# One sine product, scores ahead of values, and the softmax reciprocal spread by TensorE inside the output bank

## The chip, the cores and the metric

One Trainium2 chip, one of its cores. Five engines run their own instruction streams and meet at semaphores: TensorE (PE in the profile, its weight loads PEld), VectorE (DVE), ScalarE (ACT), GpSimd (POOL) and SyncE (SP), which issues DMAs here. The metric is the device time of the program in microseconds; lower is better.

## The reference, cut to what matters

The program is a stack of stages over 16 sequences of 256 tokens and 128 channels. The change touches the second stage, a transformer of six layers with local attention (16 heads of 64, window 32). The feed-forward half of a layer is left out here:

```python
qkv = shift_tokens(x) @ Wqkv            # x: (16, 256, 128), Wqkv: (128, 3 * 1024)
q = l2norm(q) * qs;  k = l2norm(k) * ksc
q = q * cos * scale + rotate_half(q) * sin * scale
k = k * cos * inv + rotate_half(k) * sin * inv
# windows of 32 queries see their own and the one before
sim = einsum('bhwie,bhwje->bhwij', bq, bk2) * 8
attn = softmax(where(mask, -max, sim))
out = einsum('bhwij,bhwje->bhwie', attn, bv2)
x = out @ Wo + x
x = ffn(shift_tokens(x)) + x
```

## The kernel before

Each stage (`phase_a`: first attention, `phase_b`: the six-layer transformer, `phase_c`: the state-space stage) is a software pipeline. In `phase_b` an item is one sequence in one layer, 6 x 16 = 96 items. A step of the pipeline works on four of them at once: the projection (front) of item n+1, the local attention of item n, output projection and layer norm (tail) of item n-1, the feed-forward of item n-2. A step has 16 slots, and every engine walks through them in the same order; what an engine does in a slot is written out by hand, and an engine waits only where a semaphore says so. An instruction that waits holds back all that is behind it on its engine.

Attention goes by pairs of heads, p = 0 to 7, one in each even slot. For pair p:

- slot 2p: PE `scores(p)`: the mask is put into the two score banks by a bf16 product (L799), then q times k for both heads (L803, L806). DVE takes the row maximum (L1093); ACT takes four exponentials with row sums into `ssum` (L955, L957). `scores(p)` waits for the exponentials of p-1.
- slot 2p+2: PE transposes the probabilities into `T_BANK` (L828, L829), ACT copies them to `PT` (L979); DVE turns the small block of the window before (L1089).
- slot 2p+4: PE `values(p)`: values times `PT` (L789, L793) into half of `O_BANK`; two pairs, a group, fill the bank.

The softmax denominators go by groups i of two pairs (GROUPS = 4): slot 4i+4, DVE, reciprocal of `ssum` (L1098) and its spreading to 64 columns a head, `rrep` (L1103, 128x512); slot 4i+5, PE, four transposes of `rrep` into `T_BANK` (L903); slot 4i+6, ACT, copy to `rb` (L975); slot 4i+7, DVE, `O_BANK` times `rb` into `oT` (L1084). Slots above 15 fall into the next step. So the first `values` of a group waits for the L1084 of the group before, and the probability transposes of that slot wait for the L975 that empties `T_BANK`.

In an even slot PE does, in this order, `values(p-2)`, `scores(p)`, the transposes of p-1, and then a piece of the projection of the next item (L845 to L847, 512 columns) and spare-bank work. ACT does the `rb` copy, the `PT` copy, the exponentials, and then the square of the projection piece into `sq` (L991) or its copy to `V`. DVE does L1084 (odd slots), L1089, L1093, the reciprocal work, and in the slot behind a q or k piece `rotate`: the cosine product (L1057), two half-wide sine products (L1060), the sum of squares (L1063). Pieces of q and k are in slots 1, 2, 4, 6, 8, 10, 12 and 13.

PE's other work: `WO_SLOT` 4 and 5, output projection, half in each (L859); first feed-forward product in slots 6, 8, 9 (L885), the second in slot 15 (L893); transposes of q and k in slots 10 to 13 and 0 to 3 (L776). ACT loads another function table for the GELU of slot 11 (L998) and loads the exponential's again in slot 12. DVE normalises in slots 15 and 1 (L1070).

Of the kernel before, what the change touches and what calls it, by code (L numbers as in the profile page):

```python
# [22 lines left out]
ALU = mybir.AluOpType  # L23
# [554 lines left out]
WO_SLOT = (4, 5)  # L578
# [4 lines left out]
PAIR_T, PAIR_PV = 2, 4  # L583
SPREAD_LAG, TURN_LAG, KEEP_LAG, SCALE_LAG = 4, 5, 6, 7
# [84 lines left out]
def phase_b(nc, g, d, ps):  # L669
    with ExitStack() as stack:  # L670
# [15 lines left out]
        s.rrep = s.sb("rrep", [P, TT, 4, DB]); s.rb = s.sb("rb", [P, 2, NT]); s.oT = s.sb("oT", [P, HPAIRS, NT])  # L686
# [9 lines left out]
        s.pv_done, s.rinv_ready, s.rrep_ready, s.rb_full, s.rb_ready, s.onorm = s.sems("pv_done rinv_ready rrep_ready rb_full rb_ready onorm")  # L696
# [56 lines left out]
        def _(pe):  # L753
            def body(step):
# [24 lines left out]
                def values(item, p, own):  # L779

                    pe.wait_ge(s.pt_ready, HPAIRS * item + p + 1)
                    pe.wait_ge(s.before_ready, HPAIRS * item + p + 1)
                    if p % 2 == 0:
                        wait(pe, s.onorm, GROUPS * item + p // 2)
                    pt, v = s.PT[:, p % 2], s.V[:, own]
                    at = p % 2 * NT
                    for j in range(2):
                        side, head = slice(j * DB, (j + 1) * DB), slice((2 * p + j) * DB, (2 * p + j + 1) * DB)
                        nc.tensor.matmul(ps[side, O_BANK, at:at + KEYS], v[:, 0, head], pt[:, j, 0:KEYS], start=True, stop=False,  # L789
                                         skip_group_check=True)  # L790
                    for j in range(2):
                        side, head = slice(j * DB, (j + 1) * DB), slice((2 * p + j) * DB, (2 * p + j + 1) * DB)
                        last = nc.tensor.matmul(ps[side, O_BANK, at + P:at + NT], v[:, 1, head], pt[:, j, KEYS:KEYS + P], start=False, stop=True,  # L793
                                                skip_group_check=True)
                    last.then_inc(s.pv_done, 1)
# [14 lines left out]
                for slot in range(SLOTS):  # L810
                    item, p = pair_at(step, slot, PAIR_PV)
                    if p is not None:
                        values(item, p, pa if slot >= PAIR_PV else 1 - pa)
                    elif step.attn and slot == 0:
                        for use in TRANSPOSE_SLOT.values():
                            bank, uses = step.spare_of_before(("tr", use))
                            pe.wait_ge(s.spare_free[bank], uses + 1)
                    if step.attn and slot % 2 == 0:
                        wait(pe, s.exp_done, HPAIRS * n + slot // 2)
                        scores(slot // 2)  # L820
                    item, p = pair_at(step, slot, PAIR_T)
                    if p is not None:
                        if not step.attn:
                            pe.wait_ge(s.exp_done, HPAIRS * item + p + 1)
                        if p % 2 == 0:
                            wait(pe, s.rb_ready, GROUPS * item + p // 2)
                        for j in range(2):
                            nc.tensor.transpose(ps[:, T_BANK, j * NT:j * NT + P], s.Pr[:, p % 2, j, 0:P], g.ident[:])  # L828
                            last = nc.tensor.transpose(ps[:, T_BANK, j * NT + P:(j + 1) * NT], s.Pr[:, p % 2, j, OWN], g.ident[:])  # L829
                        last.then_inc(s.t_done, 1)  # L830
# [79 lines left out]
        def _(act):  # L910
            act.wait_ge(s.zeroed, 1)

            def body(step):
# [47 lines left out]
                for slot in range(SLOTS):  # L961
# [8 lines left out]
                    item, i = group_at(step, slot, KEEP_LAG)  # L970
                    if i is not None:
                        act.wait_ge(s.rb_full, GROUPS * item + i + 1)
                        if not step.attn:
                            wait(act, s.onorm, GROUPS * item + i)
                        nc.scalar.activation(s.rb[:], ps[:, T_BANK].rearrange("p (a t) -> p a t", a=2), ACT.Copy).then_inc(s.rb_ready, 1)  # L975
# [27 lines left out]
        def _(dve):  # L1003
# [20 lines left out]
            def body(step):  # L1024
# [20 lines left out]
                def rotate(at):  # L1045
# [27 lines left out]
                for slot in range(SLOTS):  # L1073
# [5 lines left out]
                    item, i = group_at(step, slot, SCALE_LAG)  # L1079
                    if i is not None:  # L1080
                        dve.wait_ge(s.rb_ready, GROUPS * item + i + 1)
                        if not step.attn:
                            dve.wait_ge(s.pv_done, HPAIRS * item + 2 * i + 2)
# [11 lines left out]
                    item, i = group_at(step, slot, SPREAD_LAG)  # L1095
                    if i is not None:
                        heads = slice(4 * i, 4 * i + 4)
                        nc.vector.reciprocal(s.rinv[:, heads], s.ssum[:, heads]).then_inc(s.rinv_ready, 1)  # L1098
                        if not step.attn:
                            dve.wait_ge(s.rb_full, GROUPS * item + i)  # L1100
                        dve.wait_ge(s.rinv_ready, GROUPS * item + i + 1)
                        wide = s.rinv[:, heads].rearrange("p h (t o) -> p t h o", o=1).broadcast_to((P, TT, 4, DB))
                        nc.vector.tensor_tensor(s.rrep[:], wide, wide, ALU.max).then_inc(s.rrep_ready, 1)  # L1103
# [547 lines left out]
```

## Time and profile before

| | |
|---|---|
| median of 3 runs | 6295.01 us (6290.99 to 6296.99) |
| the profiled execution | 6296.2 us; its span from the first to the last instruction 6294.4 us |
| PE busy | 5301.7 us (84% of the span) |
| DVE, ACT, POOL busy | 4720.1 us (75%), 4122.9 us (66%), 3575.6 us (57%) |
| granted TensorE clock, mean | 0.941 of full speed |

Busy times are the union of an engine's instructions. Idle time of an engine counts only if what follows it on the chain that ends last came later by it. A timeline row gives the start in us from the span's start, the duration in us, engine, line and operation, what it writes and reads, and in brackets the engine's idle time ahead of it and what ended that. A matmul of f32 data is recorded as two instructions, a transpose as one; instructions of one line that follow each other are merged into one row (x4). The end of a matmul is modelled, so distances are taken from start to start.

### The profile page before, as it was taken

The numbers are of one execution on the slowest core, as the hardware profiler recorded it, in microseconds if no ns is written. First come the engines' busy times: TensorE is split into PE (matmuls) and PEld (weight loads), VectorE is DVE, ScalarE is ACT, GpSimd is POOL, SyncE is SP. The second block draws the span as 40 slices with busy tenths as digits, with TensorE's granted clock in tenths as the row PEclk, the third lists the DMA queues.
The fourth block names the chain that finished last, engine by engine and source line by source line (L and its number), as shares of the span: only waits on it lengthen the run. The fifth ranks groups of instructions, "written<-read, shape, count | busy, mean of one in ns | idle before, by whom it ended". The sixth has DMA issues, their size and how long they took to land. (4 is left out here: it accounts for less than half of the span.)

```text
span 6294.4 us, 111018 instructions
## 1 busy us (share of the span) xinstructions
PE 5301.7 (84%) x34984; PEld 3935.5 (63%) x34984; DVE 4720.1 (75%) x9586; ACT 4122.9 (66%) x12293; POOL 3575.6 (57%) x2277
## 2 busy tenths in 40 slices
PE   7999788888888888888888888888888888566666
PEld 6999666666666666666666666666666666333333
DVE  4666677777777787777777777777777776577777
ACT  3555467777777777777777777777777776454543
POOL 1222466666666666666666666666666664344444
PEclk9999899999999999999999999999999999688887
DMA  0000000000000000000000000000000000000000
GB/s 20 4 3 2 23 1 0 0 0 10 10 0 0 0 18 1 0 0 4 14 1 0 0 5 13 1 0 0 5 8 1 0 0 0 4 3 3 3 3 4
DMA packets 35417, 25.50 MB, mean 4 GB/s; under 512 B 11315, under 2 KB 29302, under 8 KB 35190
## 3 DMA queue, kind: packets, MB, share of 16 engines
q1 hardware_dynamic: 26302, 22.22, 1.2%
q8 instruction: 118, 1.93, 0.1%
q10 hardware_dynamic: 8888, 0.45, 0.1%
q14 instruction: 109, 0.89, 0.1%
HBM read 20.57 MB, written 2.10 MB: 4 GB/s over the span
## 5 line engine op out<-in xcount | busy, mean ns | idle before, releaser
L1155 POOL TENSOR_TENSOR b_w<-b_w,b_vt 128x512 f32<-128x512 f32 x768 | 986.7, 1285 | 1547.3 <-DVE b_ss L1063 1020.2
L1159 POOL TENSOR_TENSOR b_rn<-b_ssm,all_neg_half 128x16 f32<-128x16 f32 x384 | 1127.3, 2936 | 32.0
L979 ACT ACTIVATE b_PT<-ps 128x512 f32<-128x512 f32 x768 | 459.5, 598 | 978.4 <-PE ps L829 978.4
L1057 DVE TENSOR_TENSOR b_w<-ps,until_b_rotab 128x512 f32<-128x512 f32 x768 | 527.8, 687 | 648.3 <-ACT b_sq L991 643.7
L1093 DVE TENSOR_REDUCE b_nm<-ps 128x4 f32<-128x640 f32 x768 | 633.1, 824 | 235.1 <-PE ps L806 209.0
L955 ACT ACTIVATE b_Pr<-ps,b_nm 128x128 f32<-128x128 f32 x1536 | 564.4, 367 | 111.6 <-DVE b_nm L1093 109.8
L957 ACT ACTIVATE b_Pr<-ps,b_nm 128x160 f32<-128x160 f32 x1536 | 609.7, 397 | 0.0
L845 PE MATMUL ps<-b_Whi,b_xlo 128*128 128x512 f32 x1152 | 590.5, 513 | 19.0 <-DVE b_Wlo L1078 11.4
L789 PE MATMUL ps<-b_PT,b_V 128*64 128x160 f32 x3072 | 385.3, 328 | 244.9 <-DVE b_oT L1084 237.7
L1060 DVE TENSOR_TENSOR b_vt<-ps,until_b_rotab 128x256 f32<-128x256 f32 x1536 | 571.6, 413 | 0.0
L828 PE MATMUL ps<-all_ident,b_Pr 128*128 128x128 f32 x1536 | 439.1, 311 | 153.7 <-ACT b_rb L975 147.2
L1063 DVE TENSOR_REDUCE b_ss<-b_sq 128x8 f32<-128x512 f32 x768 | 517.9, 674 | 0.0
L991 ACT ACTIVATE b_sq<-ps 128x512 f32<-128x512 f32 x768 | 472.9, 616 | 12.1 <-PE ps L847 12.0
L799 PE MATMUL ps<-until_b_mask_bf,until_b_ident_bf 128*128 128x320 bf16 x1536 | 346.3, 308 | 143.9 <-ACT b_Pr L957 143.0
L776 PE MATMUL ps<-all_ident,b_w 128*128 128x128 f32 x3072 | 463.7, 280 | 3.0 <-DVE b_w L1070 3.0
L925 ACT ACTIVATE b_qkT<-ps 128x512 f32<-128x512 f32 x768 | 463.1, 621 | 0.6 <-PE ps L776 0.5
L847 PE MATMUL ps<-b_Whi,b_xhi 128*128 128x512 f32 x1152 | 460.2, 400 | 0.0
L846 PE MATMUL ps<-b_Wlo,b_xhi 128*128 128x512 f32 x1152 | 458.7, 398 | 0.0
L776 PEld LDWEIGHTS ps<-all_ident,b_w 128*128 128x128 f32 x3072 | 381.0, 145 | 96.2 <-ACT b_qkT L925 23.8
L828 PEld LDWEIGHTS ps<-all_ident,b_Pr 128*128 128x128 f32 x1536 | 222.1, 145 | 309.0 <-ACT b_rb L975 219.8
L789 PEld LDWEIGHTS ps<-b_PT,b_V 128*64 128x64 f32 x3072 | 158.7, 137 | 407.7 <-issue 348.9
L829 PE MATMUL ps<-all_ident,b_Pr 128*128 128x128 f32 x1536 | 397.0, 284 | 0.0
(256 smaller groups left out, 14155.0 us busy)
## 6 DMA issues: line engine op xcount, KB each, us to landing
b_Wraw<-in_L_ffn_Wqkv SPq DMA_DIRECT2D x36, 256.0 KB, 2.8
b_Wo<-in_L_ffn_Wo SPq DMA_DIRECT2D x6, 512.0 KB, 4.0
a_xtok<-in_L_attn_hidden_states SPq DMA_DIRECT2D x16, 128.0 KB, 2.1
out<-c_xout SPq DMA_DIRECT2D x16, 128.0 KB, 1.8
b_W<-in_L_ffn_W SPq DMA_DIRECT2D x6, 341.0 KB, 2.9
setup_wmod<-in_L_wmod SPq DMA_DIRECT2D x2, 384.0 KB
b_W<-in_L_ffn_W SPq DMA_DIRECT2D x6, 128.0 KB
setup_rot<-in_rot SPq DMA_DIRECT2D x1, 256.0 KB
```

Of the source, the lines that this page charges most:

```text
L776: last = nc.tensor.transpose(bank[:, i * P:(i + 1) * P], s.w[:, tt, c % 2, c // 2, i * P:(i + 1) * P], g.ident[:])
L789: nc.tensor.matmul(ps[side, O_BANK, at:at + KEYS], v[:, 0, head], pt[:, j, 0:KEYS], start=True, stop=False, skip_group_check=True)
L828: nc.tensor.transpose(ps[:, T_BANK, j * NT:j * NT + P], s.Pr[:, p % 2, j, 0:P], g.ident[:])
L845: nc.tensor.matmul(ps[:, F_BANK[k % 2]], s.xlo[:, pf, rows], s.Whi[:, cols], start=True, stop=False)
L955: nc.scalar.activation(s.Pr[:, p % 2, j, 0:P], ps[:, S_BANK[j], WIN:KEYS], ACT.Exp, bias=s.nm[:, h, 0:1], accum_out=s.ssum[:, h, 0:1])
L957: last = nc.scalar.activation(s.Pr[:, p % 2, j, P:], ps[:, S_BANK[j], KEYS:2 * KEYS], ACT.Exp, bias=s.nm[:, h, 1:2], accum_out=s.ssum[:, h ...
L1057: nc.vector.tensor_tensor(s.w[:, tt, c % 2, which].rearrange("p (h e) -> p h e", e=DB), rotated, g.rotab[:, bass.ds(lf, 1), 2 * which, tt] ...
L1060: last = nc.vector.tensor_tensor(turned[:, :, z], raw[:, :, 1 - z], sin[:, :, z * (DB // 2):(z + 1) * (DB // 2)].broadcast_to((P, 8, DB // ...
L1063: nc.vector.tensor_reduce(s.ss[:, j, which * 8:(which + 1) * 8], s.sq[:, i % 2].rearrange("p (h e) -> p h e", e=DB), AX.X, ALU.add).then_i ...
L1093: nc.vector.tensor_reduce(s.nm[:, 2 * p:2 * p + 2], ps[:, S_BANK[0]:S_BANK[1] + 1, 0:TT * KEYS].rearrange("p j (t k) -> p j t k", t=TT), A ...
L1155: nc.gpsimd.tensor_tensor(rows, rows, s.vt[:, i % 4], ALU.add).then_inc(s.pool_add, 1)
L1159: nc.gpsimd.tensor_tensor(s.rn[:, j], s.ssm[:, j], g.neg_half[:, 0:HB], ALU.pow).then_inc(s.pool_r, 1)
```

## The change

`scores(p)` is issued ahead of `values(p-2)` in an even slot. `O_BANK` now belongs to one pair: the values go to its columns 0 to 255, and behind them four more matmuls, two token halves by two heads, have the reciprocal's column, repeated 64 times by a step of 0, as stationary operand and the identity as moving one; they put the spread reciprocal into columns 256 to 511. For an even p they wait for the reciprocal (`rinv_ready`), which DVE makes in the same slot, now ahead of the row maximum. L1103, the L903 transposes, `rrep` and the waits on `T_BANK` for `rb` go. ACT copies `rb` for each pair (256 columns) in the slot of its values, ahead of the `PT` copy; DVE scales each pair (256 columns) in the odd slot behind. `values(p)` waits for the scaling of pair p-1. The two sine products become one of 512 columns whose PSUM operand is read with the half index reversed (a negative step). `WO_SLOT` goes from (4, 5) to (3, 4).

```diff
-WO_SLOT = (4, 5)
+WO_SLOT = (3, 4)
-PAIR_T, PAIR_PV = 2, 4
-SPREAD_LAG, TURN_LAG, KEEP_LAG, SCALE_LAG = 4, 5, 6, 7
+PAIR_T, PAIR_PV, PAIR_SCALE = 2, 4, 5
+RINV_LAG = 4
@@ PE, values(item, p, own)
-                    if p % 2 == 0:
-                        wait(pe, s.onorm, GROUPS * item + p // 2)
+                    wait(pe, s.onorm, HPAIRS * item + p)
...
+                    if p % 2 == 0:
+                        pe.wait_ge(s.rinv_ready, GROUPS * item + p // 2 + 1)
+                    for tt in range(TT):
+                        for j in range(2):
+                            side, at = slice(j * DB, (j + 1) * DB), NT + tt * P
+                            last = nc.tensor.matmul(ps[side, O_BANK, at:at + P], s.rinv[:, 2 * p + j, tt:tt + 1].broadcast_to((P, DB)), g.ident[:],
+                                                    start=True, stop=True, skip_group_check=True)
@@ PE, order in a slot
+                    if step.attn and slot % 2 == 0:
...
+                        wait(pe, s.exp_done, HPAIRS * n + slot // 2)
+                        scores(slot // 2)
                     item, p = pair_at(step, slot, PAIR_PV)
                     if p is not None:
                         values(item, p, pa if slot >= PAIR_PV else 1 - pa)
...
-                        if p % 2 == 0:
-                            wait(pe, s.rb_ready, GROUPS * item + p // 2)
...
-                            pe.wait_ge(s.onorm, GROUPS * t + 2 * half + 2)
+                            pe.wait_ge(s.onorm, HPAIRS * t + 4 * half + 4)
...
-                    item, i = group_at(step, slot, TURN_LAG)
-                    if i is not None:
-                        pe.wait_ge(s.pt_ready, HPAIRS * item + 2 * i + 2)
-                        pe.wait_ge(s.rrep_ready, GROUPS * item + i + 1)
-                        for p in range(2):
-                            for tt in range(TT):
-                                last = nc.tensor.transpose(ps[:, T_BANK, p * NT + tt * P:p * NT + (tt + 1) * P],
-                                                           s.rrep[:, tt, 2 * p:2 * p + 2].rearrange("p j e -> p (j e)"), g.ident[:])
-                        last.then_inc(s.rb_full, 1)
@@ ACT
-                        nc.scalar.activation(s.rb[:], ps[:, T_BANK].rearrange("p (a t) -> p a t", a=2), ACT.Copy).then_inc(s.rb_ready, 1)
+                    item, p = pair_at(step, slot, PAIR_PV)
+                    if p is not None:
+                        act.wait_ge(s.pv_done, HPAIRS * item + p + 1)
+                        nc.scalar.activation(s.rb[:, p % 2], ps[:, O_BANK, NT:2 * NT], ACT.Copy).then_inc(s.rb_ready, 1)
@@ DVE
-                    for z in range(2):
-                        last = nc.vector.tensor_tensor(turned[:, :, z], raw[:, :, 1 - z],
-                                                       sin[:, :, z * (DB // 2):(z + 1) * (DB // 2)].broadcast_to((P, 8, DB // 2)), ALU.mult)
-                    last.then_inc(s.dve_uv, 1)
+                    nc.vector.tensor_tensor(turned, raw[:, :, ::-1], sin.rearrange("p a (z e) -> p a z e", z=2).broadcast_to((P, 8, 2, DB // 2)),
+                                            ALU.mult).then_inc(s.dve_uv, 1)
...
-                        nc.vector.tensor_tensor(s.oT[:, 2 * i:2 * i + 2], ps[:, O_BANK].rearrange("p (a t) -> p a t", a=2), s.rb[:],
-                                                ALU.mult).then_inc(s.onorm, 1)
+                    item, p = pair_at(step, slot, PAIR_SCALE)
+                    if p is not None:
+                        dve.wait_ge(s.rb_ready, HPAIRS * item + p + 1)
+                        nc.vector.tensor_tensor(s.oT[:, p], ps[:, O_BANK, 0:NT], s.rb[:, p % 2], ALU.mult).then_inc(s.onorm, 1)
...
+                    item, i = group_at(step, slot, RINV_LAG)
+                    if i is not None:
+                        heads = slice(4 * i, 4 * i + 4)
+                        nc.vector.reciprocal(s.rinv[:, heads], s.ssum[:, heads]).then_inc(s.rinv_ready, 1)
...
-                        wide = s.rinv[:, heads].rearrange("p h (t o) -> p t h o", o=1).broadcast_to((P, TT, 4, DB))
-                        nc.vector.tensor_tensor(s.rrep[:], wide, wide, ALU.max).then_inc(s.rrep_ready, 1)
```

## Rows read from the trace of the kernel before

**Rows 1.** Busy time in the transformer stage: stretch, its length, busy us of each engine.

```profile
740.00:5356.00 4616.00, 4014.97 (x28483) 2986.45 (x28482) 3576.55 (x7751) 3320.66 (x10164) 2989.14 (x1901) 0.97 0.01 3
```

**Rows 2.** Waits of PE in the whole run: us in total, times, longest.

```profile
PE ps L789 <- DVE b_oT L1084: 237.7, 164, 3.0
...
PE ps L828 <- ACT b_rb L975: 147.2, 167, 1.3
PE ps L799 <- ACT b_Pr L957: 143.0, 98, 1.6
...
PE ps L903 <- DVE b_rrep L1103: 46.7, 59, 1.6
```

**Rows 3.** Timeline of PE, slots 10 and 12 of one step.

```profile
3061.14 0.27 PE L829 MATMUL ps<-all_ident,b_Pr 128*128 128x128 f32 x1
...
3063.61 0.49 PE L789 MATMUL ps<-b_PT,b_V 128*64 128x160 f32 x4
3063.94 0.39 PE L793 MATMUL ps<-b_PT,b_V 128*64 128x128 f32 x4
3064.26 0.44 PE L799 MATMUL ps<-until_b_mask_bf,until_b_ident_bf 128*128 128x320 bf16 x2
...
3065.33 0.33 PE L828 MATMUL ps<-all_ident,b_Pr 128*128 128x128 f32 x1
...
3065.71 0.27 PE L829 MATMUL ps<-all_ident,b_Pr 128*128 128x128 f32 x1
```

**Rows 4.** Timeline of ACT, slot 10: last of the exponentials.

```profile
3063.28 0.22 ACT L957 ACTIVATION_READ_ACCUMULATOR b_Pr<-ps,b_nm 128x1 f32 x1
```

**Rows 5.** Timeline of DVE, slots 11 and 12.

```profile
3064.11 0.69 DVE L1057 TENSOR_TENSOR b_w<-ps,until_b_rotab 128x512 f32<-128x512 f32 x1 [1.95 <-ACT b_sq L991]
3064.72 0.74 DVE L1060 TENSOR_TENSOR b_vt<-ps,until_b_rotab 128x256 f32<-128x256 f32 x2
3065.38 0.67 DVE L1063 TENSOR_REDUCE b_ss<-b_sq 128x8 f32<-128x512 f32 x1
3066.08 0.24 DVE L1089 STREAM_TRANSPOSE b_PT<-b_Pr 32x64 f32<-32x64 f32 x1
```

**Rows 6.** Timeline of PE, slots 0, 4, 6, 8 and 9.

```profile
3029.42 0.49 PE L789 MATMUL ps<-b_PT,b_V 128*64 128x160 f32 x4 [1.61 <-DVE b_oT L1084]
...
3032.09 0.42 PE L829 MATMUL ps<-all_ident,b_Pr 128*128 128x128 f32 x1
...
3040.60 0.49 PE L789 MATMUL ps<-b_PT,b_V 128*64 128x160 f32 x4 [1.34 <-DVE b_oT L1084]
...
3042.69 0.27 PE L829 MATMUL ps<-all_ident,b_Pr 128*128 128x128 f32 x1
...
3045.92 1.89 PE L859 MATMUL ps<-b_oT,b_Wo 128*128 128x256 f32 x8
...
3055.05 0.27 PE L829 MATMUL ps<-all_ident,b_Pr 128*128 128x128 f32 x1
...
3058.38 0.60 PE L903 MATMUL ps<-all_ident,b_rrep 128*128 128x128 f32 x4
```

**Rows 7.** Timeline of PE, slot 0 of the next step.

```profile
3077.24 0.49 PE L789 MATMUL ps<-b_PT,b_V 128*64 128x160 f32 x4 [1.61 <-DVE b_oT L1084]
```

**Rows 8.** Timeline of ACT, slot 12.

```profile
3067.50 0.59 ACT L979 ACTIVATE b_PT<-ps 128x512 f32<-128x512 f32 x1
...
3070.75 0.21 ACT L957 ACTIVATION_READ_ACCUMULATOR b_Pr<-ps,b_nm 128x1 f32 x1
```

**Rows 9.** Timeline of DVE, slot 0 of the next step.

```profile
3079.66 0.24 DVE L1089 STREAM_TRANSPOSE b_PT<-b_Pr 32x64 f32<-32x64 f32 x1
...
3080.68 0.19 DVE L1098 RECIPROCAL b_rinv<-b_ssum 128x8 f32<-128x8 f32 x1
```

**Rows 10.** Groups of DVE by line: count, busy us, mean ns, idle before.

```profile
L1084 DVE TENSOR_TENSOR b_oT<-ps,b_rb 128x512 f32<-128x512 f32 x384 | 261.0, 680 | 1.5 <-PE ps L793 1.5
```

**Rows 11.** Groups of ACT by line, same stretch and columns.

```profile
L946 ACT ACTIVATE b_hgate<-ps,b_lp 128x256 f32<-128x256 f32 x192 | 96.0, 500 | 11.5 <-PE ps L885 11.5
```

More of the change, by code:

```diff
@@ L685, in phase_b @@
         s.PT = s.sb("PT", [P, 2, 2, 2 * KEYS])
-        s.rrep = s.sb("rrep", [P, TT, 4, DB]); s.rb = s.sb("rb", [P, 2, NT]); s.oT = s.sb("oT", [P, HPAIRS, NT])
+        s.rb = s.sb("rb", [P, 2, NT]); s.oT = s.sb("oT", [P, HPAIRS, NT])
         s.lp = s.sb("lp", [P, 7]); s.lnp = s.sb("lnp", [P, 2])
@@ L695, in phase_b @@
             "clamp_done pool_r s_done max_done exp_done t_done pt_ready before_ready")
-        s.pv_done, s.rinv_ready, s.rrep_ready, s.rb_full, s.rb_ready, s.onorm = s.sems("pv_done rinv_ready rrep_ready rb_full rb_ready onorm")
+        s.pv_done, s.rinv_ready, s.rb_ready, s.onorm = s.sems("pv_done rinv_ready rb_ready onorm")
         s.lp_ready, s.lnp_ready, s.shifted, s.gelu_done, s.hg_ready, s.x_ready = s.sems("lp_ready lnp_ready shifted gelu_done hg_ready x_ready")
@@ L782, in values @@
                     pe.wait_ge(s.before_ready, HPAIRS * item + p + 1)
-                    if p % 2 == 0:
-                        wait(pe, s.onorm, GROUPS * item + p // 2)
+                    wait(pe, s.onorm, HPAIRS * item + p)
                     pt, v = s.PT[:, p % 2], s.V[:, own]
-                    at = p % 2 * NT
                     for j in range(2):
                         side, head = slice(j * DB, (j + 1) * DB), slice((2 * p + j) * DB, (2 * p + j + 1) * DB)
-                        nc.tensor.matmul(ps[side, O_BANK, at:at + KEYS], v[:, 0, head], pt[:, j, 0:KEYS], start=True, stop=False,
+                        nc.tensor.matmul(ps[side, O_BANK, 0:KEYS], v[:, 0, head], pt[:, j, 0:KEYS], start=True, stop=False,
                                          skip_group_check=True)
@@ L792, in values @@
                         side, head = slice(j * DB, (j + 1) * DB), slice((2 * p + j) * DB, (2 * p + j + 1) * DB)
-                        last = nc.tensor.matmul(ps[side, O_BANK, at + P:at + NT], v[:, 1, head], pt[:, j, KEYS:KEYS + P], start=False, stop=True,
-                                                skip_group_check=True)
+                        nc.tensor.matmul(ps[side, O_BANK, P:NT], v[:, 1, head], pt[:, j, KEYS:KEYS + P], start=False, stop=True,
+                                         skip_group_check=True)
+                    if p % 2 == 0:
[5 more added lines that the diff above has]
+                                                    start=True, stop=True, skip_group_check=True)
                     last.then_inc(s.pv_done, 1)
@@ L810, in body @@
                 for slot in range(SLOTS):
+                    if step.attn and slot % 2 == 0:
+                        if slot == 0 and step.tail is None:
+                            for use in TRANSPOSE_SLOT.values():
+                                bank, uses = step.spare_of_before(("tr", use))
+                                pe.wait_ge(s.spare_free[bank], uses + 1)
+                        wait(pe, s.exp_done, HPAIRS * n + slot // 2)
+                        scores(slot // 2)
                     item, p = pair_at(step, slot, PAIR_PV)
@@ L813, in body @@
                         values(item, p, pa if slot >= PAIR_PV else 1 - pa)
[L814 to L820, printed above, removed]
                     item, p = pair_at(step, slot, PAIR_T)
@@ L969, in body @@
                     read_spare(slot - 1)
[L970 to L974, printed above, removed]
-                        nc.scalar.activation(s.rb[:], ps[:, T_BANK].rearrange("p (a t) -> p a t", a=2), ACT.Copy).then_inc(s.rb_ready, 1)
+                    item, p = pair_at(step, slot, PAIR_PV)
+                    if p is not None:
+                        act.wait_ge(s.pv_done, HPAIRS * item + p + 1)
+                        nc.scalar.activation(s.rb[:, p % 2], ps[:, O_BANK, NT:2 * NT], ACT.Copy).then_inc(s.rb_ready, 1)
                     item, p = pair_at(step, slot, PAIR_T)
@@ L1078, in body @@
                             nc.vector.tensor_tensor(s.Wlo[:, cols], s.Wraw[:, k % RAW], s.Whi[:, cols].bitcast(F32), ALU.subtract).then_inc(s.w_ready, 1)
[L1079 to L1083, printed above, removed]
-                        nc.vector.tensor_tensor(s.oT[:, 2 * i:2 * i + 2], ps[:, O_BANK].rearrange("p (a t) -> p a t", a=2), s.rb[:],
-                                                ALU.mult).then_inc(s.onorm, 1)
+                    item, p = pair_at(step, slot, PAIR_SCALE)
+                    if p is not None:
+                        dve.wait_ge(s.rb_ready, HPAIRS * item + p + 1)
+                        nc.vector.tensor_tensor(s.oT[:, p], ps[:, O_BANK, 0:NT], s.rb[:, p % 2], ALU.mult).then_inc(s.onorm, 1)
                     item, p = pair_at(step, slot, PAIR_T)
@@ L1094, in body @@
                                                 AX.X, ALU.max, negate=True).then_inc(s.max_done, 1)
[L1095 to L1101, printed above, removed]
-                        wide = s.rinv[:, heads].rearrange("p h (t o) -> p t h o", o=1).broadcast_to((P, TT, 4, DB))
-                        nc.vector.tensor_tensor(s.rrep[:], wide, wide, ALU.max).then_inc(s.rrep_ready, 1)
                     if step.tail is not None and slot == RES_SLOT:
```

## The prediction

> **What bounds the kernel now.** I read the page's slices first: the transformer stage runs evenly between some 0.74 and 5.36 ms, so what happens to one of its steps happens about 94 times (96 items, the pipeline full for 94). In that stage PE is busy for 4015 of 4616 us, DVE for 3577, ACT for 3321, POOL for 2989 [rows 1]. PE is near its limit, but it does wait, and the view of waits tells for whom: the values for the scaling of the group before, 237.7 us; the transposes of the probabilities for the `rb` copy that still uses their bank, 147.2; the scores for the exponentials, 143.0; the turning of `rrep` for DVE, 46.7 [rows 2]. Together that is 575 us, 6 us a step. So there is something to win, and PE still has to be fed.
>
> Then the timeline of one whole step. From one slot-0 `values` to the next it takes 3077.24 - 3029.42 = 47.82 us [rows 6, 7]. The reader is to see how far DVE is behind PE: PE begins slot 12 at 3063.61 [rows 3], DVE gets to its first instruction of that slot, L1089, at 3066.08 [rows 5], 2.47 us later, because it had to do the rotation of slot 11 first, and that waited 1.95 us for ACT's square, which stands behind the exponentials. The same lag is in slot 0: PE at 3077.24 [rows 7], DVE at 3079.66 [rows 9]. Before the change that lag is harmless: in slot 12 PE wants from DVE only what was made in slots before.
>
> **The change part by part: PE's work.** A transpose of 128 f32 columns takes 0.11 us of PE; so L903 costs 4 x 0.11 = 0.43 a group. L793, two f32 matmuls of 128 columns in four instructions, begins 0.32 ahead of the mask; the L789 before it, with 160 columns, takes 0.33 without a change of array shape behind it, so L793's own work is 0.33 x 128/160 = some 0.21 to 0.26 (I take 0.21, two transposes' time) and 0.11 is the gap at the change from 64 stationary columns to 128 [rows 3]. The new matmuls are four of L793's kind: 2 x 0.21 = 0.43 a pair. Bounds: 0.43 if both halves of the array work side by side as L793's seem to, 0.86 if a repeated column loses that.
>
> Here a rule speaks against the change. The Trainium skill, TensorE: Matmul & The Clock Gate, section Terms, says that the transpose mode is four times faster for FP32, and the new matmuls spread the column without it. By that rule one of them would cost 4 x 0.11 = 0.44 and four, in side-by-side pairs, 0.88; the rows of L793 show a factor of two, and the sum goes by them.
>
> Order: before, an even slot changes array shape four times (values 64 columns, mask 128, scores 64 rows, transposes 128), after it three times, since values follow the scores directly: a gap of 0.11 less. PE's work a step: 8 x (0.43 - 0.11) - 4 x 0.43 = +0.8 us.
>
> **DVE and ACT.** L1103 goes, 0.69 us four times, where DVE was not late for anybody. L1084 (0.68 [rows 10]) becomes two of 256 columns, nearest the half-wide sine products, 0.33 apart: the same in all, but only one of them, some 0.28 shorter, stands in front of what follows in its slot. The single sine product should run like the 512-wide cosine product, 3064.72 - 3064.11 = 0.61 from start to start, where the two took 3065.38 - 3064.72 = 0.66 [rows 5]: 0.05 saved. The negative step is in no row; the bounds are 0 and twice the time (+0.6). I take 0.61, since the two halves already read PSUM out of order. ACT copies 256 columns eight times instead of 512 four times; nearest is L946, 0.50 [rows 11]. It stands ahead of the `PT` copy, but the transposes take longer to arrive than it, so it costs something only where ACT is late itself, in slot 12.
>
> **Waits that go, and the one that comes.** The `rb` wait of the transposes and the `rrep` wait are gone, and the scaling is wanted 1.07 us later in its slot, behind the scores. In their place PE waits, in slots 0, 4, 8 and 12, in front of the new matmuls, for a reciprocal that DVE makes in the same slot behind L1089. PE would be there 1.07 (scores, 3064.26 to 3065.33) + 0.54 (values) = 1.61 us after the start of the slot [rows 3]; DVE, at its present lag, 2.47 + 0.24 (L1089) + 0.19 (L1098 [rows 9]) + 0.08 (two starts, estimate) = 2.98 [rows 3, 5]. Behind the waiting matmul on PE are the transposes of the probabilities, behind these the `PT` copy, the exponentials, the square, the rotation, the L1089 of the next even slot, and the projection. So from such a matmul to the next it is a chain, and I price it, R being the first new matmul:
>
> - R to the last transpose: 0.43 + 0.10 + 0.38 (3065.33 to 3065.71) = 0.91. Slot start to last transpose: 1.61 + 0.91 = 2.52 [rows 3].
> - Last transpose to exponentials done: 3061.14 to 3063.28 + 0.22 = 2.36 [rows 3, 4].
> - Last transpose of a slot to the reciprocal of the next even slot seen by PE: 3066.08 - 3061.14 = 4.94, - 0.05, + 0.51 = 5.40 [rows 3, 5].
>
> Slot 0 to 4: 0.91 + 2.36 + 0.05 (the scores' start) + 2.52 + 5.40 = 11.24. The output projection's half that moves to slot 3 fits under the 5.40. Slot 4 to 8: 0.91 + PE's work up to slot 6 + 2.52 + 5.40. That work is 3042.69 to 3045.92 = 3.23 [rows 6]: the second half of the output projection, which began there, is now earlier. 12.06. Slot 8 to 12: work up to slot 10 is 3055.05 to 3058.38 = 3.33 [rows 6], 12.16. Slot 12 to 0: R at 3061.14 + 5.40 = 3066.54; ACT, held up by the GELU and two table loads, gets to the `PT` copy at 3067.50, now 0.50 later for `rb`, so its exponentials end at 3070.96 + 0.50 = 3071.46 [rows 8]; from there to L1089 of slot 0 it was 3079.66 - 3070.96 = 8.70 of DVE work [rows 8, 9], less 0.28 and 2 x 0.05, plus 0.51: R at 3080.29, 13.75. The sum is 49.21 against 47.82, +1.39 us. The table loads stay as they are.
>
> One term more: in slot 0 the transposes ran at the lower clock (0.42 long at 3032.09, 0.27 at 3065.71 [rows 3, 6]), behind a stretch of waits. With R waiting there longer, R and the transposes at half rate would add 0.43 + 0.38 = 0.81. No row says whether the slow stretch falls on them; I take half, 0.40. In all +1.79 a step, x 94 = +168 us. On the execution's own 6296.2 us, which is 1.2 above the median of the runs, that is 6464, for the median 6463; I say 6460.
>
> **Rivals.**
>
> *The waits just go (faster).* If DVE reached slots 0, 4, 8 and 12 less than 1.61 - 0.51 = 1.1 us behind PE, the new wait would be none. Then 237.7 + 147.2 + 46.7 = 432 us go, PE's work adds 0.8 x 94 = 75, the scores, no longer behind the values, wait 0.65 longer in slot 14, 61: 6296 - 296 = 6000. For it: PE's work would fill only some 42 of the 47.8 us, and DVE has 23% of the stage idle. Against it: a lag of 2.47, which waits for ACT, not for DVE's own work. It decides by degrees: each of the four chains has one 5.40 in it, and at 5.40 - 1.79 / 4 = 4.95 the change breaks even.
>
> *R is dear (much slower).* R at 0.86 is in each leg twice: 8 x 0.43 = +3.44 a step, +323: 6786. This is also the time by the skill's rule above. A sine product at half rate adds 0.6 to each rotation on the chains, 5 a step, 3.0 x 94 = +282: 6745.
>
> *The new wait equals the old (no change).* 6 us of wait before; if R's waits replace them and the 0.8 of PE's work hides under ACT's table loads, 6296.
>
> **How the numbers follow.** Chance of the chain as priced: 0.52; its own range 6380 (no slow clock, `rb` hidden, each link 0.1 shorter) to 6540 (slow clock in full, links 0.1 longer). R or the product dear: 0.15. No change: 0.06. Faster, in part or in full: 0.27, about a third of it below 6150. The range leaves that third out and the dearest cases, 6150 to 6600. 0.2%, 12.6 us, is about what a measurement of this kernel can tell from no change. Faster 0.27, same 0.06, slower 0.67.
>
> **What would show it.** In the view of waits of the changed kernel the matmul line with `rinv` as stationary operand should wait for the reciprocal on DVE in 250 or more of 384 cases, 300 us or more in all; the lines for `oT` and `rb` should be near nothing; ACT's wait for the transposes should grow. The new matmuls' starts show R: 0.43 or 0.86 for eight. One row of the sine product shows its rate. A step should be 49 to 50 us. Wrong would be: R's waits under 0.4 us each, or a step under 47.8. What I trust least is that the 4.94 stays what it is when the slots around it shift.

## The result, and the profile after

The changed kernel takes 6731.76 us (median of 4 runs, 6729.46 to 6734.77) against 6296.00 (4 runs, 6290.99 to 6297.23): 1.069 times as long, 95% interval 1.068 to 1.071. Slower was forecast, but 6460 with a range of 6150 to 6600. Of the 436 us, the prediction accounts for 168.

Line numbers move. In the changed kernel L798 are the new matmuls, L804, L808 and L811 the scores, L787 and L791 the values, L831 and L832 the transposes of the probabilities, L862 the output projection, L967 the `rb` copy, L971 the `PT` copy, L949 and L951 the exponentials, L983 the square, L919 the copy of q and k into `qkT`, L1049 and L1051 the cosine and sine products, L1072 the scaling, L1080 the reciprocal, L1084 the row maximum. In the experiments line numbers differ by a few from these; the names tell the operations (`b_rb` the `rb` copy, `b_nm` the maximum, `b_Pr` the exponentials).

The view of waits, PE, changed kernel (us in total, times, longest):

```profile
PE ps L798 <- DVE b_rinv L1080: 439.4, 287, 4.3
PE ps L804 <- ACT b_Pr L951: 222.6, 202, 3.6
...
PE ps L862 <- ACT b_qkT L919: 153.1, 95, 1.8
```

Against [rows 2]: the waits for `oT`, `rb` and `rrep` are gone but for 3 of 432 us. In their place stand the predicted wait for the reciprocal, 439 us in 287 of the 384 cases (slots 8, 12 and 0 in nearly every step, slot 4 once in all), 80 us more in front of the scores, and a wait that no part of the prediction has: the output projection waits in nearly every step for ScalarE's copy of q and k.

One step, on PE's timeline, from slot 6 to slot 6 of the next step (slots 8, 12, 14, 0, 2, 3, 4 between them; window 3000 to 3060 us):

```profile
3001.83 0.45 PE L804 MATMUL ps<-until_b_mask_bf,until_b_ident_bf 128*128 128x320 bf16 x2
...
3003.44 0.61 PE L798 MATMUL ps<-all_ident,b_rinv 128*64 128x128 f32 x8
3003.98 0.33 PE L831 MATMUL ps<-all_ident,b_Pr 128*128 128x128 f32 x1
...
3009.78 0.66 PE L798 MATMUL ps<-all_ident,b_rinv 128*64 128x128 f32 x8 [1.06 <-DVE b_rinv L1080]
...
3021.91 0.66 PE L798 MATMUL ps<-all_ident,b_rinv 128*64 128x128 f32 x8 [1.21 <-DVE b_rinv L1080]
...
3026.71 0.45 PE L804 MATMUL ps<-until_b_mask_bf,until_b_ident_bf 128*128 128x320 bf16 x2 [1.29 <-ACT b_Pr L951]
...
3035.76 0.66 PE L798 MATMUL ps<-all_ident,b_rinv 128*64 128x128 f32 x8 [2.06 <-DVE b_rinv L1080]
...
3037.03 0.42 PE L832 MATMUL ps<-all_ident,b_Pr 128*128 128x128 f32 x1
...
3040.04 0.43 PE L804 MATMUL ps<-until_b_mask_bf,until_b_ident_bf 128*128 128x320 bf16 x2
...
3042.56 0.27 PE L832 MATMUL ps<-all_ident,b_Pr 128*128 128x128 f32 x1
...
3045.94 1.99 PE L862 MATMUL ps<-b_oT,b_Wo 128*128 128x256 f32 x8 [1.52 <-ACT b_qkT L919]
...
3049.38 0.61 PE L798 MATMUL ps<-all_ident,b_rinv 128*64 128x128 f32 x8
...
3053.52 0.45 PE L804 MATMUL ps<-until_b_mask_bf,until_b_ident_bf 128*128 128x320 bf16 x2
```

The step is 3053.52 - 3001.83 = 51.69 us, where it was 47.82 [rows 6, 7]. It is one of the shorter ones: the mean over the 95 steps of the stage, from the scores of slot 0 to the next, is 52.53, and 48.07 in the kernel before. Taken from L798 to L798 in slots 8, 12, 0, 4 and 8, as the prediction did (in slot 4 it does not wait; in the last slot 8 it starts at 3061.37):

| stretch | predicted | measured |
|---|---|---|
| slot 8 to 12: 3009.78 to 3021.91 | 12.16 | 12.13 |
| slot 12 to 0: 3021.91 to 3035.76 | 13.75 | 13.85 |
| slot 0 to 4: 3035.76 to 3049.38 | 11.24, and 0.40 for the clock | 13.62 |
| slot 4 to 8: 3049.38 to 3061.37 | 12.06 | 11.99 |

Three stretches came out within 0.1 us. The fourth, slot 0 to 4, is 2 us longer, and it holds both the L862 with its wait and a stretch of long transposes (0.42 at 3037.03, 0.27 at 3042.56), that is, of the lower of the clock's two levels: the granted clock is 0.60 on the mean from 3035.76 to 3040.04, behind the wait of 2.06 us, and 1.00 from there to 3049.38.

VectorE before and in slots 7 and 8 of the same step:

```profile
3007.35 0.69 DVE L1049 TENSOR_TENSOR b_w<-ps,until_b_rotab 128x512 f32<-128x512 f32 x1 [1.20 <-ACT b_sq L983]
3007.95 0.68 DVE L1051 TENSOR_TENSOR b_vt<-ps,until_b_rotab 128x512 f32<-128x512 f32 x1
3008.55 0.68 DVE L1053 TENSOR_REDUCE b_ss<-b_sq 128x8 f32<-128x512 f32 x1
3009.26 0.24 DVE L1076 STREAM_TRANSPOSE b_PT<-b_Pr 32x64 f32<-32x64 f32 x1
3009.53 0.20 DVE L1080 RECIPROCAL b_rinv<-b_ssum 128x8 f32<-128x8 f32 x1
```

This is the chain at work: square, rotation, L1076, reciprocal at 3009.53, and L798 at 3009.78, on which the transposes wait. The sine product with the reversed index goes at 0.60 from start to start.

ScalarE, slots 2 and 3:

```profile
3044.42 0.41 ACT L951 ACTIVATE b_Pr<-ps,b_nm 128x160 f32<-128x160 f32 x1
3044.69 0.22 ACT L951 ACTIVATION_READ_ACCUMULATOR b_Pr<-ps,b_nm 128x1 f32 x1
3044.79 0.62 ACT L983 ACTIVATE b_sq<-ps 128x512 f32<-128x512 f32 x1
3045.26 1.11 ACT L919 ACTIVATE b_qkT<-ps 128x512 f32<-128x512 f32 x2
```

The transposes of q and k of slots 2 and 3 fill the two spare banks. The first bank is emptied by the first of the two L919 merged in the last row, which stands behind the exponentials and the square of slot 2. L862 in slot 3 takes that bank and starts at 3045.94. In slot 4, where the projection was, the bank had been free.

### The profile page after: what moved, and what is told of

Its sections match the earlier page's. It is cut to its first block and busy times, and to the rows that moved or that the text cites. A ratio compares the mean times of both kernels' runs of the same rounds, so it can differ in the third digit from the quotient of the medians.

```text
span 6732.9 us, 119047 instructions
## 1 busy us (share of the span) xinstructions
PE 5500.8 (82%) x39592; PEld 4174.8 (62%) x39592; DVE 4487.5 (67%) x8818; ACT 4195.9 (62%) x12677; POOL 3429.3 (51%) x2277
## 5 line engine op out<-in xcount | busy, mean ns | idle before, releaser
L1049 DVE TENSOR_TENSOR b_w<-ps,until_b_rotab 128x512 f32<-128x512 f32 x768 | 529.0, 689 | 1170.6 <-ACT b_sq L983 1170.6
L967 ACT ACTIVATE b_rb<-ps 128x256 f32<-128x256 f32 x768 | 293.5, 382 | 1390.5 <-PE ps L798 1390.5
L798 PE MATMUL ps<-all_ident,b_rinv 128*64 128x128 f32 x6144 | 513.5, 291 | 439.4 <-DVE b_rinv L1080 439.4
L1084 DVE TENSOR_REDUCE b_nm<-ps 128x4 f32<-128x640 f32 x768 | 618.4, 805 | 215.9 <-PE ps L811 206.7
L798 PEld LDWEIGHTS ps<-all_ident,b_rinv 128*64 128x64 f32 x6144 | 367.4, 144 | 508.7 <-DVE b_rinv L1080 508.7
L848 PE MATMUL ps<-b_Whi,b_xlo 128*128 128x512 f32 x1152 | 607.6, 527 | 13.9 <-DVE b_Wlo L1068 7.9
L951 ACT ACTIVATE b_Pr<-ps,b_nm 128x160 f32<-128x160 f32 x1536 | 611.8, 398 | 0.0
L949 ACT ACTIVATE b_Pr<-ps,b_nm 128x128 f32<-128x128 f32 x1536 | 564.2, 367 | 31.9 <-DVE b_nm L1084 30.3
L971 ACT ACTIVATE b_PT<-ps 128x512 f32<-128x512 f32 x768 | 459.4, 598 | 175.2 <-PE ps L832 175.2
L804 PE MATMUL ps<-until_b_mask_bf,until_b_ident_bf 128*128 128x320 bf16 x1536 | 350.3, 311 | 229.1 <-ACT b_Pr L951 222.6
L1051 DVE TENSOR_TENSOR b_vt<-ps,until_b_rotab 128x512 f32<-128x512 f32 x768 | 522.7, 681 | 0.0
L776 PE MATMUL ps<-all_ident,b_w 128*128 128x128 f32 x3072 | 507.6, 299 | 3.9 <-DVE b_w L1060 3.9
L862 PE MATMUL ps<-b_oT,b_Wo 128*128 128x256 f32 x1536 | 372.2, 385 | 153.1 <-ACT b_qkT L919 153.1
L776 PEld LDWEIGHTS ps<-all_ident,b_w 128*128 128x128 f32 x3072 | 431.8, 158 | 91.5 <-issue 16.5
L983 ACT ACTIVATE b_sq<-ps 128x512 f32<-128x512 f32 x768 | 474.2, 618 | 12.2 <-PE ps L850 12.1
L919 ACT ACTIVATE b_qkT<-ps 128x512 f32<-128x512 f32 x768 | 462.4, 620 | 0.4 <-PE ps L776 0.3
L831 PE MATMUL ps<-all_ident,b_Pr 128*128 128x128 f32 x1536 | 452.6, 318 | 0.0
```

The lines of the kernel that those rows point to most:

```text
L776: last = nc.tensor.transpose(bank[:, i * P:(i + 1) * P], s.w[:, tt, c % 2, c // 2, i * P:(i + 1) * P], g.ident[:])
L798: last = nc.tensor.matmul(ps[side, O_BANK, at:at + P], s.rinv[:, 2 * p + j, tt:tt + 1].broadcast_to((P, DB)), g.ident[:], start=True, stop ...
L848: nc.tensor.matmul(ps[:, F_BANK[k % 2]], s.xlo[:, pf, rows], s.Whi[:, cols], start=True, stop=False)
L949: nc.scalar.activation(s.Pr[:, p % 2, j, 0:P], ps[:, S_BANK[j], WIN:KEYS], ACT.Exp, bias=s.nm[:, h, 0:1], accum_out=s.ssum[:, h, 0:1])
L951: last = nc.scalar.activation(s.Pr[:, p % 2, j, P:], ps[:, S_BANK[j], KEYS:2 * KEYS], ACT.Exp, bias=s.nm[:, h, 1:2], accum_out=s.ssum[:, h ...
L983: nc.scalar.activation(s.sq[:, i % 2], ps[:, F_BANK[k % 2]], ACT.Square).then_inc(s.act_front, 1)
```

## The experiments

All against the kernel before on the same chip; ratios with their 95% interval.

**1. The reciprocal made for each pair, one even slot earlier** (label e1_rinv_per_pair), in the changed kernel:

```diff
 @@ PE, values
-                    if p % 2 == 0:
-                        pe.wait_ge(s.rinv_ready, GROUPS * item + p // 2 + 1)
+                    pe.wait_ge(s.rinv_ready, HPAIRS * item + p + 1)
 @@ DVE, slot 2p+2, right behind L1076
+                        heads = slice(2 * p, 2 * p + 2)
+                        nc.vector.reciprocal(s.rinv[:, heads], s.ssum[:, heads]).then_inc(s.rinv_ready, 1)
 @@ DVE, slot 4i+4
-                        heads = slice(4 * i, 4 * i + 4)
-                        nc.vector.reciprocal(s.rinv[:, heads], s.ssum[:, heads]).then_inc(s.rinv_ready, 1)
```

> The changed kernel with one edit: the reciprocal is made for each pair by itself, one even slot earlier (slot 2p+2, right behind L1089 of that pair, instead of slot 2p+4 for a group), so TensorE never wants it in the slot in which it is made. Theory A (the chain): the wait of the new matmuls for the reciprocal, 439 us, is what lengthens the step; without it the step falls from 51.7 us by about its waits in slots 0, 8 and 12 (2.1 + 1.0 + 1.2 = 4.2), less what the scores then wait longer for the exponentials; a step of 48 to 49 and a time of 6400 to 6500. Rival B (the lag stays, the wait moves): TensorE just arrives earlier at the scores of the next slot and waits there for the exponentials, whose own chain is as long; waits for L1080 near 0 but those for the exponentials up by 300 us or more, time 6650 to 6740. Rival C (TensorE's extra work and the spare bank decide): time within 1% of 6732 and waits small.

Measured: 6428.79 us (6422.19 to 6435.43), 1.021 (1.019 to 1.023). 303 us of the 436 are gone with this one edit, although TensorE does the same matmuls. Its waits:

```profile
PE ps L802 <- ACT b_Pr L949: 411.2, 258, 4.1
...
PE ps L860 <- ACT b_qkT L917: 153.2, 95, 2.4
```

The wait for the reciprocal is off the list. That for the exponentials rose by 189 us, in slots 14 (from 124 to 251 us) and 2 (from 4 to 108), while in slot 0 it fell from 92 to 44. So theory A holds, and rival B has a part of it: four tenths of the removed 439 us came back as waits for the exponentials. C falls.

**2. The output projection back in slots 4 and 5** (e2_wo_slots_4_5), in the changed kernel. `oT` gets a second buffer, or pair 0 of the next item would be scaled into what slot 5 still reads:

```diff
-WO_SLOT = (3, 4)
+WO_SLOT = (4, 5)
-s.oT = s.sb("oT", [P, HPAIRS, NT])
+s.oT = s.sb("oT", [P, 2, HPAIRS, NT])
 @@ PE: s.oT[:, c] -> s.oT[:, 1 - pa, c];  DVE: s.oT[:, p] -> s.oT[:, <parity of the item's step>, p]
```

> The changed kernel with the output projection back in slots 4 and 5; oT gets a second buffer, by the parity of the step, since pair 0 of the next item is now scaled into it before the projection has read it. Theory A: the wait of the projection for a spare bank (153 us, 1.5 to 1.7 in every slot 3) goes, and with it 1.4 from the stretch between slots 0 and 4, but 1.6 of projection comes back between slots 4 and 8, where TensorE's work is on the chain: 6720 to 6770, about no change. Rival: the bank wait is a plain loss, 6732 - 153 = 6580.

Measured: 6750.24 us (6747.96 to 6750.90), 1.072 (1.071 to 1.074). As theory A has it: the bank wait is gone from its list, and the time is 18 us longer. Its waits:

```profile
PE ps L798 <- DVE b_rinv L1080: 549.8, 381, 4.5
PE ps L804 <- ACT b_Pr L951: 271.2, 292, 3.6
```

What it saved there, TensorE waits for the reciprocal of slot 4 (381 waits instead of 287), and the projection stands between slots 4 and 8 again. On the mean over the steps, slot 0 to 4 went from 14.05 to 12.59 us and slot 4 to 8 from 12.16 to 13.84.

**3. Both edits** (e3_rinv_per_pair_wo_4_5).

> Both edits together: reciprocal per pair one even slot earlier, and projection in slots 4 and 5 with two buffers of oT. Theory A: with no chain through the reciprocal it no longer matters in which slot TensorE does the projection, and the bank wait's 150 us are a plain gain: 130 to 150 us under the first of these kernels, 6260 to 6370. Rival (waits only move): within 1% of the first.

Measured: 6302.07 us (6295.21 to 6309.35, 10 runs), 1.0012 (1.0002 to 1.0021). The bank wait, worth -18 us with the chain through the reciprocal in place, is worth 127 without it (6429 to 6302). That is within 7 us of the kernel before. Once nothing waits for the reciprocal or the bank, what is left of the change costs about what it gains; experiment 9 has the two sides. Its one large wait in the transformer stage is

```profile
PE ps L802 <- ACT b_Pr L949: 474.2, 365, 4.2
```

**4. Values ahead of the scores again** (e4_values_first), in the changed kernel: in an even slot `values(p-2)`, with the new matmuls, then `scores(p)`; nothing else.

> The changed kernel with values (and the new matmuls behind them) ahead of the scores again, nothing else. Theory A: TensorE reaches the wait for the reciprocal 1.07 us earlier in slots 0, 4, 8 and 12 and the scores, their maximum and exponentials come behind it: 1.07 x 3 to 4 a step later, plus a gap of 0.11 in each even slot; 6732 + 300 to 480 = 7030 to 7210. Rival (the order alone costs, because the scores' wait for the exponentials is met earlier): faster than 6732 by up to the 223 us that they wait.

Measured: 7317.56 us (7307.13 to 7329.53), 1.162 (1.160 to 1.164): slower still by 586 us, more than the 480 at most that I had worked out. Its waits:

```profile
PE ps L798 <- DVE b_rinv L1080: 676.2, 288, 4.8
PE ps L787 <- DVE b_oT L1072: 218.9, 132, 2.8
```

The wait for the reciprocal grows by 237 us, the one for `oT` is back, and the mean granted clock of the run falls from 0.932 to 0.884: with the same matmuls TensorE is busy for 5843.8 us instead of 5500.8. My estimate had nothing for the clock; that the clock makes up the whole of what it lacked is likely, but not shown apart. The order is no cause of the loss; it was holding it down.

**5 and 6. The transposes ahead of values and new matmuls** (e5_transposes_first; e6_transposes_first_rb_last), starting from the third kernel, to shorten the way to the exponentials:

```diff
 @@ PE, even slot: scores(p), transposes(p-1), then values(p-2) and the new matmuls
+                        wait(pe, s.pt_ready, HPAIRS * item + p)       # ahead of the transposes
 @@ ACT: PT copy, rb copy, exponentials (e5);  PT copy, exponentials, rb copy (e6)
 @@ DVE: the pair's reciprocal behind the row maximum instead of ahead of it
```

> The third kernel (reciprocal per pair, projection in slots 4 and 5) with the transposes of the probabilities ahead of the values and the new matmuls on TensorE, the PT copy ahead of the rb copy on ScalarE (rb still ahead of the exponentials), and the reciprocal behind the row maximum on VectorE. Theory A: what is left of TensorE's waits there, some 0.6 in slots 0, 2 and 4 and 2.65 in slot 14 a step, comes from the exponentials starting only behind scores, values, new matmuls, transposes and the copy; 1.0 to 1.1 less in that chain takes the three 0.6 waits away and 0 to 1 of the 2.65: 6302 - 94 x (1.8 to 2.5) = 6070 to 6130. Rival (VectorE's own loop through square, rotation and maximum, some 5.3 a pair, already sets the exponentials): no better than 6260.

> As the fifth, but ScalarE copies rb behind the exponentials instead of ahead of them. Theory A: the exponentials end up to 0.4 us earlier, the square, and with it the rotation on VectorE, 0 to 0.1 earlier at best: the same within 40 us of the fifth. If ScalarE waits for the new matmuls ahead of the exponentials in the fifth, this one is 50 to 100 us faster.

Measured: 6314.73 us (6308.97 to 6319.16), 1.003 (1.002 to 1.004), and 6351.53 us (6348.74 to 6353.45), 1.009 (1.007 to 1.010). Theory A's times fall, and so does the 50 to 100 us that I gave the sixth over the fifth: it is 37 slower. In the fifth, TensorE's wait for the exponentials is

```profile
PE ps L802 <- ACT b_Pr L950: 380.7, 347, 3.7
```

93 us less than in the third. But TensorE is busy for 5517.2 us instead of 5413.8, 103 more with the same matmuls. From the mask of the scores to the second product of the projection piece, first in the third kernel, then in the fifth:

```profile
3002.72 0.45 PE L802 MATMUL ps<-until_b_mask_bf,until_b_ident_bf 128*128 128x320 bf16 x2
...
3005.59 0.39 PE L847 MATMUL ps<-b_Wlo,b_xhi 128*128 128x512 f32 x1
```

```profile
3001.53 0.43 PE L802 MATMUL ps<-until_b_mask_bf,until_b_ident_bf 128*128 128x320 bf16 x2
...
3004.60 0.39 PE L848 MATMUL ps<-b_Wlo,b_xhi 128*128 128x512 f32 x1
```

The same work takes 3.07 us instead of 2.87. The new order changes array shape four times again (scores, transposes, values, projection) instead of three. So the shorter way did take wait away, and the order that made it shorter gave the same back as work; I had not put the fourth change into the expectation. ScalarE in the fifth:

```profile
ACT b_rb L971 <- PE ps L796: 388.8, 672, 1.8
...
ACT b_Pr L948 <- DVE b_nm L1079: 149.1, 270, 6.0
```

ScalarE waits for the new matmuls ahead of the exponentials, so the way was not as short as I had meant. With `rb` behind them (the sixth), ScalarE and VectorE:

```profile
ACT b_Pr L948 <- DVE b_nm L1079: 687.3, 404, 5.9
```

```profile
DVE b_oT L1071 <- ACT b_rb L973: 998.0, 574, 3.6
```

Now VectorE waits 998 us for `rb`, at the head of each odd slot, ahead of its rotation, and the exponentials wait 687 us for VectorE's maximum. The rival's loop through square, rotation and maximum fits these rows, with the `rb` copy as one link more; I did not shorten it by itself, so that it is what sets the pace there is argued, not shown.

**7. The one sine product in the kernel before** (e7_before_one_sine).

> The kernel before with the one sine product alone. By the trace of the changed kernel the product takes 681 ns with 0.60 us from start to start, against 0.66 for the two: 0.06 a rotation, 2 or 3 of which in a step stand on a chain with TensorE: 6295 - 0 to 15, no change to be seen. Rival: it moves more than that, because VectorE's start of slot 3, 7, 11, 15 decides TensorE's largest wait (237.7 us): up to -40.

Measured: 6275.90 us (6265.08 to 6278.87), 0.996 (0.995 to 0.998): 22 us faster, more than I gave it. The wait for `oT` at the start of slots 0, 4, 8 and 12 went from 237.7 us [rows 2] to

```profile
PE ps L789 <- DVE b_oT L1082: 202.3, 146, 2.9
```

which is the way that the rival named. Experiment 9 shows that it is not the only one.

**8. The order alone in the kernel before** (e8_before_scores_first):

```diff
 @@ PE, even slot
-                    values(item, p, ...)
                     scores(slot // 2)
+                    values(item, p, ...)
 @@ DVE, scaling
-                        if not step.attn:
-                            dve.wait_ge(s.pv_done, HPAIRS * item + 2 * i + 2)
+                        dve.wait_ge(s.pv_done, HPAIRS * item + 2 * i + 2)
```

> The kernel before with the scores ahead of the values alone (and a wait of VectorE's scaling for the values in every step instead of the last alone, which the new order needs). The reciprocal stays a group's, spread by VectorE and turned by transposes. Theory A: the order by itself is good, one change of array shape less in a slot (0.11 x 768 = 84 us) and the wait for oT met 1.07 us later; the transposes still wait for rb: 6295 - 80 to 250 = 6045 to 6215. Rival: the probability transposes come behind scores and values as before, so that nothing is gained but the gaps, and slot 14's wait for the exponentials grows by 0.65 x 96 = 62: 6250 to 6300.

Measured: 6214.63 us (6213.56 to 6216.88), 0.987 (0.985 to 0.989): 83 us faster, at the low end of theory A. Its waits:

```profile
PE ps L799 <- ACT b_Pr L957: 307.9, 239, 2.8
...
PE ps L903 <- DVE b_rrep L1102: 97.0, 88, 3.1
...
PE ps L828 <- ACT b_rb L975: 67.5, 239, 0.7
```

The wait for `oT` is off the list (238 us before) and that for `rb` fell by 80, but 165 us came back in front of the scores and 50 in front of the turning of `rrep`: 103 us less in all. The gap of 0.11 us that goes with one change of array shape less, 84 us in all, would be the gain by itself, and so would the waits; the runs do not tell the two apart.

**9. Order and sine product in the kernel before** (e9_before_scores_first_one_sine).

> The kernel before with the two parts of the change that gained by themselves: scores ahead of the values (0.987) and the one sine product (0.996). If they are independent, 6297 x 0.987 x 0.996 = 6191. Theory A (the sine's gain came through VectorE's start of the odd slots, where TensorE waited for oT, a wait that the new order has removed): less than the product, 6195 to 6215, the order's own time. Rival (VectorE is late for the exponentials too, by the row maximum): the full product or more, 6180 to 6195.

Measured: 6198.23 us (6194.67 to 6202.70), 0.984 (0.983 to 0.986), inside theory A's range, but only 7 us above the product of the two ratios and 16 below the order's own time: three quarters of the sine's 22 us are kept, so most of that gain did not hang on the wait for `oT`, which this order has removed already, as theory A had it. It beats both kernels, by 98 us the one before and by 534 the changed one.

Against this kernel the third (experiment 3) has the new way of spreading, with its matmuls, the split into pairs and the second `oT`, and a reciprocal that nobody waits for. It is 104 us longer, and TensorE is busy for 5413.8 us instead of 5292.8, VectorE for 4499.5 instead of 4675.1. So of the changed kernel's 534 us, 104 come with the spreading itself, and 430 with the reciprocal made in the slot of its use and the projection in slot 3.

## Why the prediction was wrong in size

Point by point, by its own steps.

- **The wait that comes.** Right. It was to be 250 or more of 384 cases and 300 us or more; it is 287 and 439. It was priced in four slots of a step and came in three, since in slot 4 TensorE was later than the reciprocal. ScalarE's wait for TensorE grew as said, but in front of the `rb` copy (1390.5 us at L967, 175.2 at L971; 978.4 and 145.5 at the two copies before). Undone by itself (experiment 1), it gives back 303 us, and no other single edit of the changed kernel gives back any.
- **The price of the new matmuls.** Right: eight instructions from 3003.44 to the transposes at 3003.98, 0.54 us, 0.43 and a gap of 0.11 (0.59 behind a wait, as at 3009.78). The rival at 0.86 falls on these rows. The Trainium skill (TensorE: Matmul & The Clock Gate, section Terms) has the transpose mode four times faster for FP32; these rows show a factor of two. The rival's time, 6786, is near the measured one for another reason, which the time alone would not have shown. It also counted R twice in the leg from slot 12 to 0, where by the prediction's own account ScalarE, not R, sets the time.
- **The sine product.** Right in the trace (0.60 start to start), and small as priced, but worth 22 us in the kernel before, not the 0 to 15 of the experiment's expectation.
- **The chain's links.** Three of four stretches within 0.1 us in the step shown, and two of them on the mean over all steps (12.16 from slot 4 to 8, 12.11 from 8 to 12). The 5.40 is met to 0.01 in the stretch from 8 to 12. From 12 to 0 two errors of a size cancel: ScalarE ended its exponentials 4.74 us behind R, not 4.92, and from there to the next R it was 9.11, not 8.83.

```profile
3026.44 0.21 ACT L951 ACTIVATION_READ_ACCUMULATOR b_Pr<-ps,b_nm 128x1 f32 x1
```

- **The step that failed:** "The output projection's half that moves to slot 3 fits under the 5.40." I counted TensorE's time and the wait for `oT`, and not the bank that `take_spare` waits for. Its release stands on ScalarE behind the exponentials of slot 2: from the last transpose of slot 2 to the L798 of slot 4 it was 3049.38 - 3042.56 = 6.82 us, not 5.40. Without the wait of 1.52 it would have been 5.30, so TensorE's work did fit, and the bank did not. On the mean over all steps it is 6.88: 1.48 us a step, 139 us in 94. Experiment 2 moves this loss out of the stretch, and shows that the other place for the projection costs as much.
- **The clock term,** mis-sized: 0.40 predicted. From R in slot 0 to the last transpose it took 3037.03 - 3035.76 = 1.27 instead of 0.91, and to the next scores 3040.04 - 3037.03 = 3.01 instead of 2.41: 0.96 in this step. The second part was missing: at the lower clock the work between the transposes and the next scores no longer hides behind the exponentials. On the mean over the steps it is 1.59, 2.89 and, through slot 2, 2.69 instead of 2.52: 1.33 in all, so 0.93 more, 87 us. The stretch from R to the next scores in three steps, with its length and, third from the end, the granted clock:

```profile
3249.61:3252.99 3.38, 2.82 (x24) 1.00 0.00 0
3035.76:3040.04 4.28, 4.28 (x24) 0.60 0.00 0
3300.32:3305.26 4.94, 4.94 (x23) 0.50 0.00 2
```

  At 1.00 it is the predicted 3.32 to 0.06, but only 5 of 95 steps are so; in 35 the clock is 0.50 to 0.55, in 55 between 0.55 and 0.70. This term was not undone by itself.
- **One step taken for all.** From slot 12 to 0 the mean is 14.19 instead of 13.75: 0.44, 41 us. In nearly every second step (44 times, 24 us) VectorE starts the new step later, because its L1035 waits 0.67 us for L1115. In the kernel before that happened as often (45 times, 24 us), and nobody waited for it:

```profile
3510.26 0.47 DVE L1115 SCALAR_TENSOR_TENSOR all_xT<-ps,b_lp,all_xT 128x256 f32 x1
3511.41 0.17 DVE L1035 TENSOR_SCALAR b_lp<-until_b_lparam 128x7 f32 x1 [0.67 <-DVE all_xT L1115]
3511.64 0.24 DVE L1076 STREAM_TRANSPOSE b_PT<-b_Pr 32x64 f32<-32x64 f32 x1
3511.91 0.20 DVE L1080 RECIPROCAL b_rinv<-b_ssum 128x8 f32<-128x8 f32 x1
```

```profile
3512.17 1.12 PE L798 MATMUL ps<-all_ident,b_rinv 128*64 128x128 f32 x8 [2.62 <-DVE b_rinv L1080]
```

  The wait is 2.62 us there, 2.06 in the other steps, and the stretch 14.4 instead of 13.85. In nine steps where a layer ends or begins the stretch is 15.4 or 17.0; the longest wait of the list, 4.3 us, is of one of these.
- **The sum.** 1.48 + 0.93 + 0.44 and 0.05 in the other two stretches are 2.90 us a step over the 49.61 of the prediction (49.21 and the 0.40), 273 us in 94. The steps of the kernel before were on the mean 0.25 longer than the one that the prediction started from, which takes 23 back: 168 + 273 - 23 = 418 of the 436 us. The rest lies outside these steps and was not followed.
- **The rivals.** "The waits just go" was half in reach, only not in this kernel: with the reciprocal a slot earlier and the projection where it was (experiment 3) 6302 came out, not 6000, since the waits for the exponentials, 474 us where they had been 143, took their place. So its price counted as gained what was only moved.

## What to carry to other kernels

Ask of each wait in which slot its producer makes the value, and how far that engine is behind the consumer at that place: a value made in the slot in which it is used costs the whole lag; made one even slot earlier it was waited for no more, which gave back 303 us of time for 439 us of wait, since other waits grew. When a step is moved, list every wait in it, the buffers that it takes as well as the data that it reads, and who frees them behind what. And take a change of several parts apart before judging it: here two of its parts gain 98 us together, and the one that saved VectorE a big instruction costs 104 with everything placed well, and 534 as it was placed.

## What the runs showed of the hardware

- An f32 operand with a step of 0 as stationary and one with a negative step as input of VectorE cost no more than plain ones: L798 two instructions for 128 columns, eight in 0.43 us with both halves of the array at work; L1051, 128x512 with the reversed index, 0.60 us from start to start, as L1049 beside it.
- An f32 matmul cost here twice a transpose of as many columns. L862 of the changed kernel, four matmuls of 256 columns on the whole array, takes 1.83 us to the next scores (3045.94 to 3047.77), some 0.23 for each 128 columns; a transpose of 128 columns takes 0.11. Four matmuls of 128 columns on 64 stationary ones took 0.43 in all, so they ran in pairs side by side.
- A change of array shape cost some 0.1 us of TensorE. In the kernel before, from the last transpose of L903 to a values matmul on 64 stationary columns it was 0.20 us on the median; with the scores first (experiment 8), from the same transpose to the mask on 128 columns, 0.11.
- In the fourth experiment the same matmuls with more waits between them ran at a mean granted clock of 0.884 instead of 0.932; TensorE was busy for 343 us more, and the run was 106 us longer than the most that the waits alone were worked out to cost.
